# Reading a chunk of a recurrent decoder layer on crossed quarters of the matmul array, issued in turn with an inverse's last product

## What is computed

```python
mem = DECAY * mem + sdt
hard = (mem > THR)
spike = sur + stop_gradient(hard - sur)
mem = mem - spike * THR
alpha = sigmoid(abt + alpha_spike * spike)
beta = sigmoid(bbt[..., None] + sum(spike * beta_spike, axis=-1, keepdims=True))
...
s = s * alpha[..., None]
u = einsum('bhd,bhdv->bhv', kt, s)
s = s - beta[..., None] * einsum('bhd,bhv->bhdv', kt, u)
s = s + beta[..., None] * einsum('bhd,bhv->bhdv', kt, vt)
out = einsum('bhdv,bhd->bhv', s, qt)
```

## Time and profile before

| | us |
|---|---|
| median of 3 runs | 1095.92 |
| lowest, highest | 1093.65, 1096.85 |
| the profiled execution | 1096.75 |
| its span, first to last instruction | 1095.0 |

### The profile page before, as it was taken

How to read it: one execution, slowest core, us unless ns; L and a number is a source line. 1 busy time by engine, 2 the same in 40 slices (tenths; PEclk the granted TensorE clock), 3 DMA queues, 4 the chain that set the end, 5 groups by cost and what they waited for, 6 DMA issues and landing times. The chain is left out here.

```text
span 1095.0 us, 40049 instructions
## 1 busy us (share of the span) xinstructions
PE 972.4 (89%) x16722; PEld 648.9 (59%) x16722; DVE 698.6 (64%) x2514; ACT 482.7 (44%) x1378; POOL 208.7 (19%) x394
## 2 busy tenths in 40 slices
PE   7878768999998999999999888679999999999996
PEld 2333247777777777777777777446446546546542
DVE  2887886989889888898877765145424524714710
ACT  7667412555555555545555555313323423423311
POOL 7100201122122121221221220221210310310300
PEclk8999956999999999999999999889999999999999
DMA  3000000000000000000000000211000000100100
GB/s 97 0 1 1 1 1 3 4 4 4 4 4 4 4 4 4 4 4 4 4 5 11 22 4 4 96 37 27 7 1 21 24 1 15 27 1 3 31 1 10
DMA packets 18652, 13.83 MB, mean 13 GB/s; under 512 B 2491, under 2 KB 17259, under 8 KB 18475
## 3 DMA queue, kind: packets, MB, share of 16 engines
q1 hardware_dynamic: 18475, 11.28, 3.5%
HBM read 7.70 MB, written 1.05 MB: 8 GB/s over the span
## 5 line engine op out<-in xcount | busy, mean ns | idle before, releaser
L935 PE MATMUL banks<-work 64*64 64x64 f32 x3072 | 97.9, 234 | 24.9 <-DVE gates L674 12.9
L994 PE MATMUL banks<-work 64*64 64x32 f32 x2560 | 107.6, 224 | 5.8 <-ACT work L1351 5.0
L1285 ACT COPY work<-banks 128x128 f32<-128x128 f32 x160 | 42.8, 268 | 157.8 <-PE banks L970 157.7
L199 DVE SCALAR_TENSOR_TENSOR gates<-mom,gates 128x16 f32<-128x16 f32 x512 | 101.1, 197 | 9.5 <-ACT gates L1258 4.5
L203 DVE SCALAR_TENSOR_TENSOR mom<-gates 128x16 f32<-128x16 f32 x512 | 102.9, 201 | 5.0
L994 PEld LDWEIGHTS banks<-work 64*64 64x64 f32 x2560 | 92.5, 139 | 18.1 <-issue 10.0
L637 DVE COPY_PREDICATED gates<-work,banks 128x256 f32<-128x256 uint32 x192 | 101.9, 531 | 1.1
L935 PEld LDWEIGHTS banks<-work 64*64 64x64 f32 x3072 | 73.0, 139 | 43.2 <-issue 20.5
L531 POOL TENSOR_TENSOR mom<-mom 128x4 f32<-128x4 f32 x32 | 7.2, 223 | 384.4 <-ACT work L1330 384.4
L608 DVE TENSOR_TENSOR work<-work 128x256 f32<-128x256 f32 x160 | 67.8, 424 | 19.3 <-PE banks L935 18.7
L647 DVE TENSOR_TENSOR work<-work,banks 128x128 f32<-128x128 f32 x160 | 45.6, 285 | 48.4 <-PE banks L994 45.4
(11 more groups left out here) (263 smaller groups left out, 2140.8 us busy)
## 6 DMA issues: line engine op xcount, KB each, us to landing
work<-gates SPq DMA_DIRECT2D x28, 38.5 KB
qT<-in_x_dram SPq DMA_DIRECT2D x4, 256.0 KB, 3.8
work<-in_x_dram SPq DMA_DIRECT2D x4, 256.0 KB, 2.9
out_dram<-work SPq DMA_DIRECT2D x4, 256.0 KB, 2.3
gates<-in_w_ff_dram SPq DMA_DIRECT2D x3, 256.0 KB, 3.2
wv_sb<-in_wv_dram SPq DMA_DIRECT2D x1, 512.0 KB, 4.6
work<-in_w_out_dram SPq DMA_DIRECT2D x1, 512.0 KB, 4.0
gates<-in_x_Wq_dram SPq DMA_DIRECT2D x1, 512.0 KB, 5.0
```

Of the source, the lines that this page charges most:

```text
L199: ve.scalar_tensor_tensor(mem[:, :, t], neg_mem, -0.9, mem[:, :, t], ALU.mult, ALU.add).then_inc(charged, 1)
L935: last = pe.matmul(level_out(l)[to, a], KS[rows, n.two, hp], late[rows, hp], start=True, stop=True)
L994: last = pe.matmul(packed(psXT, l)[rows, a], Z[rows, l - 1, z], second_half(XT[:, n.two], l)[rows, a], start=True, stop=True)
L1285: ac.copy(first_half(Z[:, l - 1], l), packed(psZX_half, l)).then_inc(z_ok, 1)
```

## The change

Five edits.

1. Read of the chunk writes to the other half of the partitions: `to_out` takes the place of `to_time`, in read_state and in the read. So the read uses the crossed quarters, and read_state starts with the crossed ones and ends with the straight ones.
2. Where both `cur` and `nxt` exist (31 bodies), the read is no longer behind turn_start. Its eight products are issued in turn with the eight of the fifth XT product, with the waits of both ahead, that for o_old behind the first XT product. The body without `nxt` keeps the old place.
3. On VectorE, step 4: scaling the query of `aft2` (line 594) and two scan operations go ahead of add_xt(4), and the scan operations that stood around prefix, suffix and keep move up by one or two places.
4. The waits on kq_ok are renumbered, since the scaling of the query now counts ahead of prefix(4) and no longer behind it.
5. The projection of the outputs (front_out) takes the exchanged halves of kT and qT.

No instruction is added or taken away, apart from the places of waits.

```diff
+        def to_out(par, hp):
+            return head_rows[1 - hp // 2], 2 * par + hp % 2
...
+        def prefixed(n, l):
+            early = l == LEVELS - 1 and n.it + 1 < ROUNDS
+            return n.it * NKQ + l + 1 + early
...
-                    ve.wait_ge(kq_ok, n.it * NKQ + l + 1)
+                    ve.wait_ge(kq_ok, prefixed(n, l))
...
                         spike(scan, h + 1)
+                        if l == 4 and aft2:
+                            scale_query(aft2)
+                        if l == 4:
+                            spike(scan, h + 2)
+                            spike(scan, h + 3)
                         if nxt:
                             add_xt(nxt, l)
                         if l == 4 and gate:
                             drive(gate)
-                        spike(scan, h + 2)
+                        spike(scan, h + (4 if l == 4 else 2))
                         if aft:
                             prefix(aft, l)
-                        spike(scan, h + 3)
+                        spike(scan, h + (5 if l == 4 else 3))
                         if aft:
                             suffix(aft, l)
-                        spike(scan, h + 4)
+                        if l != 4:
+                            spike(scan, h + 4)
                         if aft:
                             keep(aft, l)
-                        spike(scan, h + 5)
+                        if l != 4:
+                            spike(scan, h + 5)
...
-                        if l == 4 and aft2:
-                            scale_query(aft2)
...
-                            (rows, hp), (to, a) = from_head(par, hp), to_time(par, hp)
+                            (rows, hp), (to, a) = from_head(par, hp), to_out(par, hp)
...
+                def read_head(n, head):
+                    (to, o), (rows, a), (_, q) = to_out(*head), at_level(*head), at_x(*head)
+                    return pe.matmul(o_out[to, o], EA[rows, n.three, LEVELS, a], U[rows, q, :],
+                                     start=False, stop=True, skip_group_check=True)
...
+                def make_xt_and_read(n, cur, gate):
+                    l = NINV
+                    if gate:
+                        pe.wait_ge(zal_ok, gate.n + 1)
+                    pe.wait_ge(z_ok, n.it * NINV + l)
+                    pe.wait_ge(xt_ok, n.it * NINV + l - 1)
+                    pe.wait_ge(e_ok, (cur.it + 1) * LEVELS)
+                    pe.wait_ge(u_ok, cur.it + 1)
+                    for i, (turn, read) in enumerate(zip(straight, halves)):
+                        (rows, a), (_, z) = at_xt(*turn), at_z(*turn)
+                        last = pe.matmul(packed(psXT, l)[rows, a], Z[rows, l - 1, z],
+                                         second_half(XT[:, n.two], l)[rows, a], start=True, stop=True)
+                        if i == len(straight) - 1:
+                            last.then_inc(xt_mm, 1)
+                        if i == 0:
+                            pe.wait_ge(o_old, cur.it + 1)
+                        last = read_head(cur, read)
                     last.then_inc(o_mm, 1)
...
-                        if nxt:
+                        if nxt and cur and l == NINV:
+                            make_xt_and_read(nxt, cur, gate)
+                        elif nxt:
                             make_xt(nxt, l, gate, gate_old)
...
-                    if cur:
+                    if cur and not nxt:
                         read_chunk(cur)
...
-                        last = pe.matmul(bank[4][:, :], wout_sb[:, h, :], (qT, kT)[h % 2][:, h // 2, row(b)],
+                        last = pe.matmul(bank[4][:, :], wout_sb[:, h, :], (qT, kT)[h % 2][:, h // 2 ^ 2, row(b)],
```

More of the change, by code:

```diff
@@ L919, in level @@
                         pe.wait_ge(qk_ok, NQK)
-                    pe.wait_ge(kq_ok, n.it * NKQ + l + 1)
+                    pe.wait_ge(kq_ok, prefixed(n, l))
                     if l == 0:
@@ L1071, in read_chunk @@
                     for head in halves:
-                        (rows, o), (_, a), (_, q) = to_time(*head), at_level(*head), at_x(*head)
-                        last = pe.matmul(o_out[rows, o], EA[rows, n.three, LEVELS, a], U[rows, q, :],
-                                         start=False, stop=True, skip_group_check=True)
+                        last = read_head(n, head)
+                    last.then_inc(o_mm, 1)
+                def make_xt_and_read(n, cur, gate):
[15 more added lines that the diff above has]
+                        last = read_head(cur, read)
                     last.then_inc(o_mm, 1)
```

## The result

| | before | changed |
|---|---|---|
| median, us | 1094.79 (4 runs, 1093.45 to 1096.85) | 1106.57 (4 runs, 1101.68 to 1110.34) |
| the profiled execution, us | 1096.75 | 1101.68 |
| its span, us | 1095.0 | 1099.9 |

The account below looks back on a forecast made before the run. Bound by the chain alpha, level(5), prefix(5), keep(5), L930, with read_chunk free in a gap. Scan rounds +6.1, gates only +2.8, neither +5.2, VectorE's order -0.3: +13.8 us, forecast 1110 us, range 1099 to 1120.

Parts of the forecast that it names:

- Worth 0: TensorE's tail: taking out read_chunk's 1.04 us saves 0, since TensorE waits for keep(5) there; at most 0.1 in the last five.
- The merged block: Reads in turn with the fifth XT product: level(5) ends 1.43 us after read_state, +0.29 in a scan round.
- the wake-up: TensorE's new wait for read_state's end (o_old): 0.10 us before the reads start.
- 0.88 and 0.40: Merged block: 0.88 us for the reads on two quarters, then 0.40 to the end of level(5)'s half on the crossed quarters.
- The rule of the Trainium skill: Weight loads overlap matmuls only across different row groups, which would stretch the merged block; the sum would be the second rival's, 1124.
- predicted +0.29: Scan round: level(5) ends at 447.53 instead of 447.24, delaying the round by 0.29 us, times 21 is +6.1.
- The other kinds: Rounds without scan: level(5) later by 0.69 us in 4 with gates only (+2.8), 1.03 in 5 with neither (+5.2).
- VectorE's order "at 0": Step 4 on VectorE: earlier alpha is worth 0 in the 21 scan rounds, as the reads hold level(5) past alpha anyway.
- by itself 10 us: Step 4 on VectorE: alpha 0.53 us earlier would by itself free level(5) by 0.5 us in 21 rounds, 10 us.
- what delays level(5) delays the round by as much: Scan rounds: TensorE idles at most 0.2 us at a time after L930, so level(5)'s delay passes whole to the round.
- the third rival: TensorE's "issue" stalls (16.5 us, 49 cases): longer idle lets late instructions catch up, 1093 to 1099, named 1097; chance 0.07.
- forecast term of 1.03 per round: Five rounds with neither scan nor gates: level(5) ends at 660.15 instead of 659.12, +1.03 us each, +5.2 in all.

Follow-up runs that it names:

- e1: Kernel before with only VectorE's new order of step 4, reads left in the tail on their old quarters; 1088.67 us, ratio 0.9932.
- e5: Changed kernel with all eight XT products ahead of the wait and the eight reads behind it, instead of in turn; 1106.11 us, ratio 1.0053.
- e2: Changed kernel with VectorE's old order, reads still in turn with the XT product; 1106.0 us, ratio 1.0088.
- e4: Changed kernel measured and traced a second time, nothing altered; 1107.51 us, ratio 1.0095.
- e10: Kernel before with only VectorE's new order of step 4, measured and traced a second time; 1087.26 us, ratio 0.9891.
- e7: Kernel with only VectorE's new order, plus keep ahead of the suffix and two scan operations in step 5; 1089.59 us, ratio 0.9894.
- e8: Changed kernel with turn_start's 16 passes issued three times over, in TensorE's idle gap; 1113.69 us, ratio 1.0111.
- e6: Changed kernel with six of the eight reads left out in the 31 merged blocks, the wait kept; 1099.78 us, ratio 0.9993.

## Why the prediction was right, and where it was off

**The tail.** "Worth 0": read_chunk was hidden, by 0.30 us in the scan rounds. e1 shows it still hidden with the chain 0.54 us shorter. Shown.

**The merged block.** Predicted 0.10 for the wake-up, 0.05 for the weights, 0.88 and 0.40, in all 1.43 us from read_state's end to level(5)'s. Measured 1.39. The wake-up and weights together were 0.06 instead of 0.15, so I had them two to three times too large. Reads at 0.11 per pair were right but for the second pair, which starts 0.16 after the first, so the block is 0.06 longer than in the tail, in e5 as well. The two errors partly cancel, and that is luck. That the XT products run beside the reads on the other quarters was right, too: 0.83 us from first to last read in the changed kernel, 0.82 in e5, where none of them has to share. The rule of the Trainium skill that spoke against the change (TensorE: Matmul & The Clock Gate, Part 3: weight loads overlap only between different row groups) is not what this trace shows: reads and XT passes of the same row half alternate here at full pace.

**The step to VectorE.** I took prefix(5) to follow level(5)'s end. In the scan rounds add_xt(5) and a scan operation come between, since XT's signal is seen only 0.04 us after the last read's end, a term that I hadn't got: 0.11 us between 444.83 and 444.94 instead of 0.06. With level(5) a little early this cancels. Prefix(5) moved from 1.20 to 1.50 after read_state, +0.30, and L930 by +0.28; predicted +0.29.

**The other kinds.** L930 moved by 0.62 (predicted 0.69) and 0.93 (1.03), from 1.93 and 1.62 to 2.55. Right within a tenth.

**VectorE's order "at 0".** e2 against e4: right, e2 is 1.5 us below, with intervals that cover each other. And "by itself 10 us" in 21 rounds: e1 and e10 gave 8.7 and 10.1 us in the medians, but only 6.7 and 7.6 of it in those rounds. That the whole comes near 10 is partly luck.

**The step that was off** is the sentence that what delays level(5) delays the round by as much. In the scan rounds L930 moved by 0.28 us in the median and by 0.35 and 0.33 in the mean of the two traces, 7.2 and 6.8 us in 21 rounds, and the stage grew by 3.9 and 3.6: the stretch behind L930 became 0.16 us shorter, 14.17 for 14.33. 4 times 0.62 is 2.5, and that stage grew by 0.9 and 0.7. That is the third rival at work, at part of its price: I gave it 0.07 as an all-or-nothing case, with 10.5 us to be absorbed. It absorbed 3.3 us in the scan rounds, about as much as the late loads became less (6.3 us before, 3.3 now), and 1.6 in the next four. e7 and e8 show it from both sides: gain 0.39 us ahead of L930 and lose it all behind it, add 64 hidden instructions and pay 0.3 us behind it. I had read the holds of the earlier trace rows as a sum of 16.5 us under one name; most of that sum is regular and stays (17.0 in the changed kernel). The ones that matter are irregular, and are found only by laying rounds over one another.

**The five last rounds agree by luck.** They grew by 3.9 and 4.7 us, where 5 times 0.93 is 4.7. But both traces of the changed kernel spend 10.2 us of them at half clock, and the one of before 3.4. e1 and e10 are one kernel, with 0 and 6.8 us at half clock there, and take 72.7 and 75.1: an estimate of 0.35 us per us at half clock from these two rows leaves 1.5 and 2.3 us for the change. The first and the last of the five are at full clock in the first trace of either kernel: 15.48 for 15.23 us, and 12.74 for 12.39. So 0.25 and 0.35 us of the 0.93 arrived. e5, with no half clock there, is 2.5 us above the kernel before, 3.7 by the same estimate, so the spread is wide; in no case did the forecast term of 1.03 per round arrive whole.

**The sum.** +13.8 us predicted, +11.8 in the medians and 0.9% (0.54 to 1.25) as a ratio, which is 9.9 us (5.9 to 13.7). The stages of the two traces of the changed kernel give +8.7 and +9.0 us for the 30 rounds, where the terms said 14.1; by the estimate above, some 2.4 us of what was measured are the clock. So the direction, the place and the sizes up to L930 were right, the sum was some 4 us too large, and the median of 1106.57 is as near to 1110 as it is partly by chance.

**Open.** Whether the last five rounds' half clock (10.2 us in the changed kernel's traces, 3.4 in the one of before) comes from the longer gaps. The traces of the other kernels have between 0 and 10 us with either order, so I call it chance, but twelve traces don't settle it. Why XT's signal is seen only with the reads' end is not shown either. A kernel with fewer instructions on TensorE, which e7 asks for, was not tried.

**Which version is best.** VectorE's order alone: 0.9932 and 0.9891 of the kernel before. e7 (0.9894) can't be told from it.

## What to carry to other kernels

Before you merge a block into another to save its time, look at what ends the wait behind it: work in a gap is free, and the same work ahead of a step that others wait for costs its whole array time, however well it overlaps. A semaphore wait in an in-order queue also holds back everything behind it: seven products that didn't need it came 0.27 us later in e6, and it went unseen only where the reads took longer still. And when a chain is shortened on an engine with a long unrolled program, measure how much arrives at the end of the round: here the instructions themselves seem to set the pace from some point on.

## What was not expected of the hardware

- TensorE resumed 0.06 us after the modelled end of its own matmuls, when it waited for a semaphore that they set. ScalarE needed 0.10 us for the same signal.
- An XT product that had ended by the model was signalled 0.35 us later, 0.04 us after the end of the reads issued around it. With the reads issued behind it (e5), the signal came 0.04 us after its own end.
- Instructions of TensorE are late by hundreds of nanoseconds in a steady loop, once per several rounds by up to 1.07 us, and the delay ends 1.25 to 1.56 us after the end of a packet of the instruction queue in 15 of 22 cases before and 45 of 98 in four other traces. 64 more instructions beside 936 per round, all in idle time, cost 0.4 us per round of 17.
- The first read_state ended anywhere from 188.0 to 195.4 us, in kernels that differ little up to there. Between 135 and 200 us TensorE's granted clock stands at half (1.2 GHz) for 27 to 48 us: 30.7 us of it in the trace that begins its rounds at 188.0, 47.8 us in those of 194.9 and 195.4, and in one of 191.1. The engine was then between the preparation and the first rounds, with idle between its blocks. Two traces of one kernel differ as much: 188.0 and 192.3 for the changed one, 189.5 and 195.4 for e1 and e10. So this is chance, up to 7 us over all traces, as much as half of what was to be measured, and it made the changed kernel's profiled execution look 5 us better than its median.
